# Groups of ten edge columns instead of nine, and the product's row built by a copy and two adds

## The reference

```python
def _L0_gnn_ref(x, edge_index, W1, b1, W2, b2, W3, b3):
    h = x @ W1 + b1
    h_i, h_j = h[dst], h[src]
    m = relu(concatenate([h_i, h_j - h_i], -1) @ W2 + b2)
    m = relu(m @ W3 + b3)
    return relu(segment_max(m, dst))

def _gat_conv(x, W, att_src, att_dst, bias, src, dst, n_nodes):
    h = x @ W
    e = leaky((h @ att_src)[src] + (h @ att_dst)[dst])      # slope 0.2
    ex = exp(e - segment_max(e, dst)[dst])
    alpha = ex / segment_sum(ex, dst)[dst]
    return segment_sum(alpha[:, None] * h[src], dst) + bias

x = layernorm(x + _L0_gnn_ref(x, ...))
x = layernorm(x + relu(_gat_conv(relu(_gat_conv(x, ...)), ...)))   # with self loops
```

## Time and profile before

| | before |
|---|---|
| median of 3 runs | 6072.81 us (6068.34 to 6073.45) |
| profiled execution, its own time | 6073.45 us |
| its span in the profile | 6072.2 us |
| busy: PE, DVE, ACT, POOL | 74%, 61%, 40%, 75% |
| mean granted TensorE clock | 0.903 |
| gathers of the attention layers (L450) | 2784 |
| matmuls of the products (L1184) | 9576 + 7182 = 342 products of 49 |
| gathers of layer 0, of layer 1 | from 2291.5 us, from 4206.7 us |
| last gather of layer 1 | 5962.4 us |

### The profile page before, as it was taken

How to read it: one execution, slowest core, us unless ns; L and a number is a source line. 1 busy time by engine, 2 the same in 40 slices (tenths; PEclk the granted TensorE clock), 3 DMA queues, 4 the chain that set the end, 5 groups by cost and what they waited for, 6 DMA issues and landing times.

```text
span 6072.2 us, 94525 instructions
## 1 busy us (share of the span) xinstructions
PE 4486.6 (74%) x25906; PEld 2886.1 (48%) x25906; DVE 3704.5 (61%) x10623; ACT 2443.7 (40%) x7395; POOL 4526.2 (75%) x4719
## 2 busy tenths in 40 slices
PE   3577777777777746888888888853888888888881
PEld 2465666566565533444444444432444444444441
DVE  3233333333333346888888788864888888888886
ACT  1122222222222244555555555533555555555554
POOL 5777777777777777777777777767777777777775
PEclk8788888888888868999999999976999999999996
DMA  5688888888888824444444444432444444444443
GB/s 130 163 228 217 214 208 208 210 210 208 213 207 211 203 70 103 122 120 120 120 120 120 119 120 120 120 98 60 120 119 120 120 120 121 121 121 120 119 120 82
DMA packets 779197, 875.07 MB, mean 144 GB/s; under 512 B 128800, under 2 KB 609525, under 8 KB 778670
## 3 DMA queue, kind: packets, MB, share of 16 engines
q1 hardware_dynamic: 622590, 559.81, 32.7%
q0 software_dynamic: 150304, 304.49, 24.1%
q10 hardware_dynamic: 5776, 4.74, 0.2%
HBM read 536.77 MB, written 331.81 MB: 143 GB/s over the span
## 4 chain that ended last, share of the span: by engine, by line
POOL 47%; PE 24%; issue 23%; DVE 2%; DMA 2%; ACT 1%; SPq 0%; POOLq 0%; DVEq 0%; ACTq 0%
POOL ring_a L450 40%; PE ps L1116 7%; PE ps L1117 6%; PE ps L1127 6%; PE ps L1137 3%; POOL ring_a L417 2%; POOL ad_edges L425 2%; POOL ring_a L391 2%; DMA ring_a<-H_table,src_i 1%; DVE ring_b L923 1%; POOL P_compact L403 1%; ACT ring_a L592 1%; PE ps L1184 0%; PE ps L1082 0%; DMA Q_table<-ring_b 0%
## 5 line engine op out<-in xcount | busy, mean ns | idle before, releaser
L450 POOL DMA_INDIRECT ring_a<-H_table,src_i x2784 | 2662.6, 956 | 848.4 <-issue 835.6
L1184 PE MATMUL ps<-work,ring_a 128*128 128x390 bf16 x9576 | 1710.4, 336 | 626.8 <-DVE ring_a L877 626.6
L391 POOL DMA_INDIRECT ring_a<-Q_table,src_i x1563 | 1488.5, 952 | 504.6 <-issue 471.6
L1184 PEld LDWEIGHTS ps<-work,ring_a 128*128 128x128 bf16 x9576 | 908.0, 99 | 1423.3 <-issue 701.1
L792 DVE TENSOR_TENSOR_SCAN work<-tab_flat,work,ps 128x512 f32<-128x512 bf16 x390 | 498.9, 1279 | 1274.3 <-PE ps L1127 1271.3
L1184 PE MATMUL ps<-work,ring_b 128*128 128x390 bf16 x7182 | 1254.0, 329 | 0.0
L923 DVE SCALAR_TENSOR_TENSOR ring_b<-ring_b,gc,ring_a 128x129 f32<-128x129 f32 x3124 | 1102.5, 353 | 155.6 <-ACT ring_a L592 129.9
L1116 PE MATMUL ps<-ident,ring_a 128*128 128x128 f32 x3126 | 702.2, 311 | 497.0 <-issue 466.4
L578 ACT ACTIVATE code<-src_row,code_bias 128x128 int16<-128x128 int32 x2052 | 636.7, 389 | 990.8 <-DVE ring_b L877 928.9
L592 ACT ACTIVATE ring_a<-ring_a,ge 128x129 f32<-128x129 f32 x3126 | 955.2, 390 | 11.4
L1184 PEld LDWEIGHTS ps<-work,ring_b 128*128 128x128 bf16 x7182 | 702.2, 98 | 497.6
(11 more groups left out here) (236 smaller groups left out, 2488.1 us busy)
## 6 DMA issues: line engine op xcount, KB each, us to landing
run_sum<-ring_b SPq DMA_DIRECT2D x346, 585.0 KB, 3.4
work<-P_compact SPq DMA_DIRECT2D x1563, 64.0 KB
tab_flat<-rank_rows SPq DMA_DIRECT2D x194, 512.0 KB
run_max<-ring_b SPq DMA_DIRECT2D x194, 512.0 KB, 4.0
ring_a<-H_table,src_i POOLq DMA_INDIRECT x2784
ring_a<-Q_table,src_i POOLq DMA_INDIRECT x1563
src_row<-in_srcL SPq DMA_DIRECT2D x342, 64.0 KB
H_table<-tab_flat SPq DMA_DIRECT2D x14, 455.0 KB, 4.1
```

Of the source, the lines that this page charges most:

```text
L391: pool.indirect_dma_start(out=q_ring[:, g % RING, j - j0, :], out_offset=None, in_=Q_table, in_offset=bass.IndirectOffsetOnAxis(ap=srcT_i[ ...
L450: pool.indirect_dma_start(out=h_ring[:, g % RING1, j - j0, :], out_offset=None, in_=H_table, in_offset=bass.IndirectOffsetOnAxis(ap=src_i[ ...
L1184: m = tensor.matmul(ps[g % 2][:, 0:3 * W], lhsT=hot_space[c // 4][:, c % 4, k - k0, :], rhs=split[:, k, :, :].rearrange("p s f -> p (s f)" ...
```

## The change

`G1` is 10 instead of 9, so that of each full group nine columns are gathered and the tenth is made by the product. The row of the product, which one reduce on DVE put together from the three parts in PSUM, is now put together in three steps: ACT copies the first part into the slot (`put_row`, called for group g+1 behind the eighth scaling of group g), and DVE adds the second part and then the third to it, the second add behind a wait for the first. `put_row` waits for the product (`picked`) and for the slot; DVE's `add_parts` waits for `put_row`'s new semaphore. The places of `add_parts` and `code_of`, which were tied to the last column by `G1 - 1`, are written as 9, which is again the last column.

```diff
-    G1, RING1, PIECE = 9, 3, 7
+    G1, RING1, PIECE = 10, 3, 7
...
+                def put_row(g):
+                    if g >= RING1:
+                        scalar.wait_ge(summed, layer * L + groups1[g - RING1][1])
+                    scalar.wait_ge(picked, (layer * NPICK + picks[g] + 1) * PIECES)
+                    scalar.activation(h_ring[:, g % RING1, G1 - 1, :], ps[g % 2][:, 0:W], ACT.Copy).then_inc(row_put, 1)
+
...
-                        if g + 3 in picks and i == G1 - 1:
+                        if g + 1 in picks and i == 7:
+                            put_row(g + 1)
+                        if g + 3 in picks and i == 9:
                             code_of(g + 3)
...
                 def add_parts(g):
                     at = layer * NPICK + picks[g]
-                    parts = ps[g % 2][:, 0:3 * W].rearrange("p (s f) -> p f s", s=3)
-                    vector.wait_ge(picked, (at + 1) * PIECES)
-                    vector.tensor_reduce(h_ring[:, g % RING1, G1 - 1, :], parts, AX_X, ALU.add).then_inc(row_added, 1)
+                    row = h_ring[:, g % RING1, G1 - 1, :]
+                    vector.wait_ge(row_put, at + 1)
+                    vector.tensor_tensor(row, row, ps[g % 2][:, W:2 * W], ALU.add).then_inc(dve.up(), 1)
+                    vector.wait_ge(dve.sem, dve.n)
+                    vector.tensor_tensor(row, row, ps[g % 2][:, 2 * W:3 * W], ALU.add).then_inc(row_added, 1)
...
-                        if g + 1 in picks and i == G1 - 1:
+                        if g + 1 in picks and i == 9:
                             add_parts(g + 1)
```

More of the change, by code:

```diff
@@ L245, in edge_network @@
             sem(n) for n in ("split_high", "split_rest", "split_mid", "split_low"))
-        coded, hot_made, picked, row_added, blocks_put = (
-            sem(n) for n in ("coded", "hot_made", "picked", "row_added", "blocks_put"))
+        coded, hot_made, picked, row_put, row_added, blocks_put = (
+            sem(n) for n in ("coded", "hot_made", "picked", "row_put", "row_added", "blocks_put"))
         scores_made, scores_exped, scaled, summed, mm_made = (
```

## The result

The changed kernel takes 6110.35 us in the median of four runs (6109.68 to 6115.42), beside 6072.42 us for the kernel before: a ratio of 1.0066, 95% interval 1.0054 to 1.0080. It is 0.7% slower, 38 us where 42 were forecast, and lies inside the range of 6086 to 6144 us.

What follows compares the result with a forecast made beforehand. POOL's gathers, their count times their pitch plus what follows the last one, were taken to bound the kernel. The sum was 6073.45 + 45.3 (gathers) - 3.5 (tails) = 6115 us, 0.7% slower, range 6086 to 6144 us.

Steps and rivals of the forecast that it cites:

- The pace: POOL in the attention layers: gathers run back to back, never held by the ring, one each 1.2583 us.
- The first rival: POOL held back by its ring of slots, so fewer groups pay off: -146 us, 5927 us; chance 0.02.
- 36 gathers at 1.2583 us, +45.3: POOL, two attention layers: 18 more gathers in each, all on the path at the steady pitch, +45.3 us.
- The tails, -3.5: Each layer's end, last gather to DVE's last column: 1.8 us less per layer from different rest groups, -3.5 us in all.
- The row at nothing: ACT's copy and DVE's two adds replacing the reduce: DVE's group 9.2 us, hidden under the 11.32 us period, no cost.
- The fourth rival: The row's added steps late, by the copy's wait or serial adds: 306 us per microsecond beyond the slack; chance 0.02.
- The forecast slack of the copy, 5 us: ACT: the next group's product ends at +10.2 us, ACT reaches the copy at +15.4, so 5 us to spare.
- the second slack: The ring's: DVE ends a group at +11.9 us, POOL wants its slot again at +22.6, 10.7 us to spare.
- The second rival: TensorE's clock falls as PE's pauses grow; decides only if products exceed 11.32 us, at worst about 7500 us; chance 0.03.
- The disturbance at no change: DVE's L923 slowing gathers, 0.010 us of the mean pitch: taken as unchanged; gone -29 us, doubled +29 us, chance 0.07 together.

Runs made afterwards that it cites:

- the 36 spare gathers: The kernel before with 18 more gathers in each layer, into a tile nobody reads; ratio 1.0065 to the kernel before, 39.7 us slower.
- the run of the row alone: Groups of 9 as in the kernel before, with the row built by the copy on ACT and two adds on DVE; ratio 1.0001 to the kernel before.
- the two runs with less work or more clock on PE: The changed kernel with 28 of 49 matmuls per product, ratio 1.0068 to before; and with SP's store of a group's sums held back three columns, 1.0071.

## Why the prediction was right

**The pace.** POOL's queue of gathers sets the end of both kernels: shown by the waits of 0.3 us, by the 36 spare gathers that cost what the changed kernel costs, and by the groups of 7, where a POOL that is held reads quite otherwise. The first rival, groups as the pace, falls: groups of 8 are more groups and faster.

**36 gathers at 1.2583 us, +45.3.** Measured 42.7 us. The count was exact. The steady pitch of the first attention layer was 1.2580; the rest of the difference is the mean over all gathers, 3553.7 / 2820 = 1.2602 us against 3511.0 / 2784 = 1.2611. That part lies in layer 1, where the pitch from the first to the last gather is 1.2602 instead of 1.2622 us; in layer 0 it is 1.2601 in both.

**The tails, -3.5.** Measured -2.9. In layer 1 the last rest of 5 was scanned 3.3 us behind its last gather and not 2.7.

**The row at nothing.** DVE's group takes 3516.40 - 3507.36 = 9.0 us in the changed kernel, 9.2 forecast; the adds take 0.29 us each, the lower end. The fourth rival falls with the run of the row alone.

The forecast slack of the copy, 5 us, was wrong. It was worked out for scans that follow each other evenly. With late scans in turn, the time from a product's last matmul to its copy ran from 0.1 to 7.9 us in layer 0. The tightest of both layers, 0.1 us, has the product's last 21 matmuls and the copy at

```profile
4447.98 3.67 PE L1194 MATMUL ps<-work,ring_b 128*128 128x390 bf16 x21
...
4451.74 0.28 ACT L586 ACTIVATE ring_a<-ps 128x130 f32<-128x130 f32 x1
```

Three copies began 0.34 to 0.38 us behind the start of the scaling before them, where 0.29 is usual. A later copy would still have had the second slack, which held: between DVE's last column of a group and the gather that takes its slot there were never less than 9.2 us in layer 0, where 10.7 were forecast. As the prediction says, only a delay beyond both would cost anything.

**The clock.** The second rival's first half came true: the granted clock of the stretch fell from 0.98 to 0.88, and a product took 1140.05 / 123.2 = 9.3 us. Its mean pause was 260.0 / 123 = 2.1 us, not 3.0, but uneven, up to 4 us and more. As reasoned, it stayed under 11.32 us (the longest of the 306 took 11.23), and the two runs with less work or more clock on PE have the same time. The Trainium skill, TensorE: Matmul & The Clock Gate, on HAM oscillation, describes such bursts that start cold, and the trace agrees: a product's first 28 matmuls took 7.50 us at 3522.67, after a pause of 4.04 us, where 4.84 is usual. It costs nothing here, because the gathers set the pace.

**The disturbance at no change.** Right in its result and by luck in its reason. I argued from the constant count of L923. Groups of 8 have that same count and a pitch of 1.2657 us, beside 1.2613 with groups of 9 on their chip. The changed kernel with the store held back has it too, and its pitch is (1062.8 + 338.6) / 1111 = 1.2614 us instead of 1.2580. What counts is where an L923 stands when a gather starts, which moves with the rhythm of the groups: in the steady stretch 147 gathers were over 0.97 us with groups of 8, 112 with 9 and 105 with 10. With 10 it happened to be nearly as with 9. I also set aside the Trainium skill's rule (SBUF — State Buffer, who interferes with whom: a DVE instruction with two SBUF inputs contends with a GpSimd instruction that reads SBUF) because of its price. The runs agree with it: a gather that is held waits until L923 ends. Its price is 0.10 us on average in the trace of before and not the 0.35 of the whole instruction, as a held gather meets L923 when part of it is over, and most gathers meet none or are not held.

## What to carry to other kernels

When one engine never waits, count its instructions before and after a change, and take the times of the others only to see whether they stay under its period. A larger group looks like less overhead, but here each group's one free column was the gain, so that the smallest group that the next engine could keep up with was the best: 8, since at 7 the products of 8.18 us took over. And where the bound is a queue of gathers on POOL, an operand of a frequent DVE instruction in PSUM instead of SBUF was worth 0.5% with groups of 9.

## What the runs showed that I had not expected

- SP's store of 650 KB, issued 0.27 us behind the last gather of a group, made the group's scan come 5.3 us behind that gather; with a store at 0.74 us (585 KB, groups of 9) it came at 2.85 us. With the store moved away the scans came at 2.6 us.
- Such a delay keeps itself going, as I read the timeline: a late group's work fills DVE until the next is long landed, its store then falls on the gather after, and scans alternate between 9.2 and 12 to 14 us. With the store held back the alternation was gone; the steps between were not tested one by one.
- A gather that a running L923 held took 1.00 to 1.12 us instead of 0.94, longer by just what was left of L923 0.13 us after the gather's start. With one of L923's operands in PSUM not one was over 0.97 us in the steady stretch.
- 49 matmuls of 390 columns back to back take 8.18 us at a granted clock of 1.00.
